# Moving four shared-expert products of one mixture stage behind its tile loop, and their output products into the next stage's routing

## What is computed

```python
# f0: 8 experts of width 176, 2 chosen per token, shared expert of width 352
scores = sigmoid(X @ gate_w.T);  _, idx = top_k(scores + router_bias, 2)
w = take(scores, idx) / sum;     out = sum_e gate[:, e] * (silu(X@W1[e]) * (X@W3[e])) @ W2[e]
out += (silu(X @ sw1.T) * (X @ sw3.T)) @ sw2.T        # the shared expert, for all tokens
x = x + 0.5 * f0(layernorm(x))
# h: gate = sigmoid(f); state scan along the sequence; x = x + (g * rms * norm * silu-like(o)) @ Wo
# f1: as f0 with 16 experts of width 128 and a shared expert of width 128
```

## Time and profile before

| what | us |
|---|---|
| three runs | 949.8, 949.8, 943.32 |
| their median | 949.8 |
| the profiled execution | 945.97 |
| span of its trace | 944.1 |
| mean granted PE clock of that span | 0.924 |

### The profile page before, as it was taken

How to read it: one execution, slowest core, us unless ns; L and a number is a source line. 1 busy time by engine, 2 the same in 40 slices (tenths; PEclk the granted TensorE clock), 3 DMA queues, 4 the chain that set the end, 5 groups by cost and what they waited for, 6 DMA issues and landing times.

```text
span 944.1 us, 14250 instructions
## 1 busy us (share of the span) xinstructions
PE 787.2 (83%) x3838; PEld 546.5 (58%) x3838; DVE 500.4 (53%) x1733; ACT 415.8 (44%) x1021; POOL 300.9 (32%) x312
## 2 busy tenths in 40 slices
PE   5899999978798899899963788895889985789892
PEld 2346677654464347677641367784667664367772
DVE  3656222277765556222287642238777776642238
ACT  3622333325643622334345244452657776145550
POOL 0562433400000651434306624450030033624550
PEclk9999999989998999999975798997899998799997
DMA  8734233199999223232293243436000011244428
GB/s 290 228 117 124 95 100 97 62 325 360 343 342 321 78 84 106 95 113 84 77 384 130 91 148 120 129 111 197 0 1 2 1 46 45 89 145 125 150 95 278
DMA packets 102363, 135.24 MB, mean 143 GB/s; under 512 B 11366, under 2 KB 90726, under 8 KB 101734
## 3 DMA queue, kind: packets, MB, share of 16 engines
q1 hardware_dynamic: 87894, 95.05, 31.4%
q0 software_dynamic: 14400, 39.34, 11.8%
HBM read 56.23 MB, written 78.12 MB: 142 GB/s over the span
## 4 chain that ended last, share of the span: by engine, by line
PE 62%; DVE 11%; issue 8%; ACT 6%; POOL 4%; DMA 4%; another core or an unknown queue 4%; SPq 2%; DVEq 0%; POOLq 0%; ACTq 0%
PE bank L980 18%; PE bank L1001 11%; PE bank L883 5%; PE bank L1050 5%; PE bank L960 4%; PE bank L991 3%; POOL slot_rows L497 3%; PE bank L1099 2%; PE bank L823 2%; PE bank L1140 2%; DVE X L1269 1%; PE bank L1167 1%; PE bank L1125 1%; DVE X L1273 1%
## 5 line engine op out<-in xcount | busy, mean ns | idle before, releaser
L497 POOL DMA_INDIRECT f_result_rows<-arena x172 | 164.8, 958 | 256.3 <-ACT arena L641 157.4
L497 POOL DMA_INDIRECT slot_rows<-XN,slots x128 | 126.1, 985 | 313.7 <-DVE slots L1383 248.7
L980 PE MATMUL bank<-w,arena 128*128 x688 | 208.7, 426 | 0.1
L1582 DVE COPY arena<-bank 88x128 f32<-88x128 f32 (+1 forms) x250 | 65.2, 285 | 249.2 <-PE bank L991 210.0
L980 PEld LDWEIGHTS bank<-w,arena 128*128 128x128 f32 x688 | 132.8, 195 | 32.6 <-issue 1.8
L1001 PE MATMUL bank<-w,arena 88*128 (+1 forms) x500 | 139.7, 388 | 0.0
L883 PE MATMUL bank<-XT,f_s 128*128 128x512 f32 (+1 forms) x256 | 127.8, 651 | 3.4 <-DMA f_s<-in_f_s 1.8
L635 ACT ACTIVATE arena<-bank 128x128 f32<-128x128 f32 (+1 forms) x172 | 50.8, 295 | 122.3 <-PE bank L980 85.9
L641 ACT ACTIVATE arena<-bank 128x256 f32<-128x256 f32 x172 | 66.0, 383 | 82.9 <-PE bank L1001 68.2
L883 PEld LDWEIGHTS bank<-XT,f_s 128*128 128x128 f32 (+1 forms) x256 | 49.9, 203 | 64.9 <-issue 60.5
L1001 PEld LDWEIGHTS bank<-w,arena 88*128 88x128 f32 (+1 forms) x500 | 82.4, 193 | 5.8 <-issue 0.8
(11 more groups left out here) (158 smaller groups left out, 1056.8 us busy)
## 6 DMA issues: line engine op xcount, KB each, us to landing
slot_rows<-zeros SPq DMA_DIRECT2D x16, 2176.0 KB, 17.9
arena<-slot_rows SPq DMA_DIRECT2D x172, 128.0 KB
XN<-f_result_rows SPq DMA_DIRECT2D x32, 256.0 KB, 5.3
Y<-f_result_rows SPq DMA_DIRECT2D x32, 256.0 KB, 6.1
w<-in_f_w SPq DMA_DIRECT2D x1, 4096.0 KB
w<-in_f_w SPq DMA_DIRECT2D x1, 2816.0 KB
f_result_rows<-arena POOLq DMA_INDIRECT x172
X<-in_x SPq DMA_DIRECT2D x4, 512.0 KB, 5.6
```

Source lines behind the costliest of these rows:

```text
L497: pool.indirect_dma_start(out=dst, out_offset=bass.IndirectOffsetOnAxis(ap=idx, axis=0), in_=src, in_offset=None).then_inc(done.sem, 16)
L980: last = pe.matmul(bank[2 + q % 2][:, 0:2 * m.H], xsT[q % 2][:, k, :], L["w13"][:, k, bass.ds(e, 1), :], start=(k == 0), stop=(k == KD - 1))
L1582: last = dve.tensor_copy(hT[q % 2][0:kp, k, :], bank[4 + q % 2][0:kp, k * P:(k + 1) * P])
```

## The change

Four edits, nothing else; no arithmetic is left out or added.

1. The second wide stage (the one whose next stage is narrow: `spread(s)`) makes pairs 8 to 10 after the tile loop too, so that pairs 8 to 11 stand there. Groups 2 and 3 get banks of their own for their output.
2. The output products of groups 2 and 3 of that stage move into the routing of the narrow stage that follows: PE makes them right after it has turned back the logits of groups 0 and 1. DVE adds them just before it combines groups 2 and 3.
3. POOL's waits in that stage: `up(8)` in place of `up(9)`, and `down(2)` in place of `down(4)`.
4. At the end of both wide stages DVE makes `weights()` before it multiplies the held pairs; before the recurrence the adds of groups 2 and 3 both stand after group 0's results have been combined. ACT's table for the square root is asked for by an instruction of its own at the start of the recurrence, and group 0's transposes there go through two banks.

```diff
-        HELD_UP = {len(MOE0.KS): 11, len(MOE1.KS): NG}
+        def spread(s):
+            return s["kind"] == "f0" and s["next"]["kind"] == "f1"
+        def held_up(s):
+            return NG if s["kind"] == "f1" else 8 if spread(s) else 11
         def down_bank(s, g, half):
             held = g - HELD[s["kind"]]
+            if spread(s) and held >= 0:
+                return bank[2 + held + 2 * half]
@@ in_turn (POOL)
-                        pool.wait_ge(*s["up"](9))
+                        pool.wait_ge(*s["up"](8 if spread(s) else 9))
-                        pool.wait_ge(*s["down"](GT))
+                        pool.wait_ge(*s["down"](2 if spread(s) else GT))
@@ recurrence (ACT)
+                act.activation(unused[:, :], epsc[:, :], ACT.Sqrt)
                 loaded(act, "h")
-                    copy_xT(s, 0, t, banks=1)
+                    copy_xT(s, 0, t, banks=2)
@@ mixture (PE)
                     logits_back(s, g)
                     if nk == 1:
+                        if s["prev"]["mixes"] and HELD["f0"] + g < NG:
+                            shared_down(s["prev"], HELD["f0"] + g)
                         positions(s, g)
-                    shared_up(2 * NG)
+                    if not spread(s):
+                        shared_up(2 * NG)
                     tile_lists()
                     pe.wait_ge(*s["experts"](1))
-                    shared_down(0)
-                    shared_up(2 * NG + 1)
-                    shared_up(2 * NG + 2)
-                    shared_down(1)
+                    shared_down(s, 0)
+                    if not spread(s):
+                        shared_up(2 * NG + 1)
+                        shared_up(2 * NG + 2)
+                    shared_down(s, 1)
...
-                for n in range(HELD_UP[nk], NG * nk):
+                for n in range(held_up(s), NG * nk):
                     shared_up(n)
-                for g in range(HELD[s["kind"]], NG):
-                    shared_down(g)
+                if not spread(s):
+                    for g in range(HELD[s["kind"]], NG):
+                        shared_down(s, g)
@@ combine (DVE)
-                if g == late:
-                    shared_add(s, NG - 1)
+                if spread(s):
+                    if g >= HELD["f0"]:
+                        shared_add(s, g)
+                elif g == late:
+                    for held in range(HELD["f0"] if s["kind"] == "f0" else NG - 1, NG):
+                        shared_add(s, held)
@@ mixture (DVE), after the tile loop
-                shared_hidden(HELD_UP[nk], NG * nk)
                 weights()
-                for g in range(HELD[s["kind"]], NG - 1):
-                    shared_add(s, g)
+                shared_hidden(held_up(s), NG * nk)
+                if nk == 1:
+                    for g in range(NG - 1):
+                        shared_add(s, g)
```

More of the change, by code:

```diff
@@ L619, in mixture @@
                 made_already = 2 * NG - 2 if nk > 1 else 0
-                for n in range(made_already, HELD_UP[nk]):
+                for n in range(made_already, held_up(s)):
                     shared_silu(n)
@@ L869, in positions, with shared_down @@
                 last.then_inc(s["pos_psum"].sem, 1)
+            def shared_down(s, g):
+                L = LAYERS[s["kind"]]
+                m = L["m"]
+                nk = len(m.KS)
+                pe.wait_ge(*s["hid"](nk * (g + 1)))
+                for h in range(2):
+                    if g >= HELD[s["kind"]] + 2:
+                        pe.wait_ge(*s["shared_added"](GT * (g - 2) + 2 * (h + 1)))
+                    elif 0 < g < HELD[s["kind"]]:
+                        pe.wait_ge(*s["shared_added"](GT * (g - 1) + 2 * (h + 1)))
+                    for t in (2 * h, 2 * h + 1):
+                        for c, kp in enumerate(m.KS):
+                            last = pe.matmul(down_bank(s, g, h)[:, t % 2 * D:(t % 2 + 1) * D],
+                                             f_HT[0:kp, (g * nk + c) % HTS, t * P:(t + 1) * P],
+                                             L["s2"][0:kp, c, :], start=(c == 0), stop=(c == nk - 1))
+                        last.then_inc(s["down"].sem, 1)
             def mixture(s):
@@ L885, in shared_up @@
                     last.then_inc(s["up"].sem, 1)
[L887 to L899, removed]
                 def tile_lists():
@@ L929, in mixture @@
                         loaded(pe, s["kind"] + "_shared")
-                        if s["prev"] is not None and s["prev"]["mixes"]:
-                            pe.wait_ge(*s["prev"]["shared_added"](NTT))
                     if nk > 1:
@@ L1037, in transpose_group @@
                     for t in range(GT):
-                        transpose_x(s, g, t, banks=1)
+                        transpose_x(s, g, t, banks=2)
                 def project(g):
@@ L1551, in mixture @@
                 if nk > 1:
-                    shared_hidden(2 * NG, 2 * NG + 1)
+                    if not spread(s):
+                        shared_hidden(2 * NG, 2 * NG + 1)
                     copy_lists()
@@ L1556, in mixture @@
                     shared_add(s, 0)
-                    shared_hidden(2 * NG + 1, 2 * NG + 2)
+                    if not spread(s):
+                        shared_hidden(2 * NG + 1, 2 * NG + 2)
                     mark(0, 0, NTT)
-                    shared_hidden(2 * NG + 2, 2 * NG + 3)
+                    if not spread(s):
+                        shared_hidden(2 * NG + 2, 2 * NG + 3)
                     shared_add(s, 1)
```

2 lines of the change are left out of this document (added).

## The result

The changed kernel took 955.11 us in the median of 20 runs (944.79 to 959.42), the kernel before 946.11 (939.73 to 950.67). The ratio is 1.0089, 95% interval 1.0069 to 1.0110: slower by 8.4 us (6.5 to 10.4), within what was predicted. The ratio is taken over fast runs alone, which leaves out two slow ones of the changed kernel (959.1 and 959.42). The join to the narrow stage costs more than the join to the recurrence gives.

What follows compares the result with a forecast made beforehand. Bound by chains of waits at three short places (overall 62% PE, 11% DVE); -2.6 + 1.0 + 9.2 = +7.6 us gave 953.6 from the profiled execution, 957.4 from the median; 955 taken, range 946 to 962.

Steps and rivals of the forecast that it cites:

- The sum: Whole kernel: -2.6 at the recurrence, +1.0 at the routing's end, +9.2 at the narrow stage, together +7.6 us.
- signals seen at once: Rival, chance 0.22: POOL's gate opens at 349.8, PE stays warm, ACT sees its logits in time; +3.2, or 951.
- Held pairs, +5.8: Join to the narrow stage: DVE combines group 0 at 481.4, not 475.65, since all four multiplications stand ahead.
- Output product in the gap, +3.4: Narrow stage: group 2's output takes 7.8 from a cold start, so counting the places comes 3.4 later.
- Adds and the third choice: Narrow stage: group 2's adds shift the second choice by 10.6; of DVE's 3.97 idle, shift becomes 8.0 to 10.4.
- +9.2 at the loop: Join to the narrow stage in all: 9.2 later, bounds 8.0 and 13, with no slack in the rest of the routing.
- Join to the recurrence, -2.6: First wide stage to recurrence: combine 0.4 earlier, table load 1.3 off the chain, projections 2.8 earlier; 2.6 kept, bounds 0.4 and 4.
- End of the routing, +1.0: Second wide stage: POOL sees its gate late, PE idles and may start the loop cold; loss 1.0, bounds -2.2 to +2.5.
- Group 3's output in the way too: Rival, chance 0.17: that product runs cold inside POOL's burst in the narrow stage and slows DVE's choice; +12.9, or 961.
- Faster than before: Rival, chance 0.08: the second wide stage's loop begins without a late-signal wait and the gate opens at once; -1.9, or 944.

Runs made afterwards that it cites:

- the kernel without POOL's wait: Changed kernel without POOL's wait for half of the second output product ahead of the last group's third tile, second wide stage: ratio 1.0073 to the kernel before.
- the second trace: The kernel before and the changed kernel, each run again with no edit, one execution each: 939.5 and 947.1.
- The same routing without the join: Changed kernel with the edits at the join to the recurrence undone: ratio 1.0117 to the kernel before.
- the kernel that takes results first: Changed kernel, DVE taking group 0's results and statistics ahead of the multiplies of pairs 10 and 11 behind the second wide stage: ratio 1.0036 to before.
- the join's kernel: Kernel before with the edits at the join to the recurrence alone: ratio 1.001; with the wait for the clearing split as well: 0.9960.
- the first ten traces: Traces of the kernel before, the changed kernel and variants of both, taken on chips other than that of the last four; no time of their own as a set.
- the last four traces: Four kernels on another chip: results first (ratio 1.0036), no POOL wait (1.0073), and two with the clearing split (0.9960, 0.9964).
- The two parts of the first join, run alone: Kernel before with only DVE's new order at the join to the recurrence, or only the early table load; one execution each, projection at 19.8 and 19.5.

## Why the prediction was right, point by point

- **The sum.** +7.6 forecast, +6.6 in the traces, +8.4 measured (6.5 to 10.4). The number came, but not by the forecast's case in full. At three places the two traces show what the rival *signals seen at once* named: POOL's gate opened 0.28 behind PE's half output, PE stayed warm, and ACT saw the third group's logits 0.4 and 1.5 late, not 4.1. That rival's sum was +3.2; the traces missed it by 2.1 in the first part, where the join's gain did not arrive, and by 1.3 in the second. So the sum owes something to misses that cancel. The 955 does too: it was the middle of 953.6 and 957.4, and the median of before turned out 3.7 lower than the three runs showed.
- **Held pairs, +5.8.** +5.7 at the combine, for the reason given: all multiplications stand ahead of it on DVE. Moving the pairs back gave back 7 us; DVE's results ahead of two of them alone gave 3.4 (0.3 to 6.5), against the kernel without POOL's wait in the same runs.
- **Output product in the gap, +3.4.** Mis-sized: places came 7.9 later than before against their loop, so 2.2. I took the cold row of 526.57 whole, but in 485 to 490 the granted clock was back to 0.75. The Trainium skill, "TensorE: Matmul & The Clock Gate", section "HAM oscillation — how this bites in real kernels", advises against matrix work in pieces between waits. The traces agree in direction: 8.30 and 7.05 us for the first product, 5.36 for the second.
- **Adds and the third choice.** Right in its low case. The sum of these rows is 9.3 at the second choice (10.6 forecast) and 6.7 at the third (8.0 to 10.4, less the same 1.3): ACT saw its logits nearly in time, so the 3.97 of DVE's idle time went, less the 1.4 of group 3's adds. On these chips it is no chance of one trace: the third group's copy came 4.1 to 4.5 behind PE's logits in the six traces with both outputs behind the loop, 0.3 to 1.5 in the four with the outputs in the gaps.
- **+9.2 at the loop.** It measured 9.3, of which only 6.8 stands at the last slot scatter. The other 2.5 arises between it and the loop and is not firmly the change's: two kernels with the narrow stage of before, one execution each, had 8.2 there as well. The term was right by this addition.
- **Join to the recurrence, -2.6.** Mis-sized twice. The combine gained 2.9, not 0.4: I put the results' landing at 195.8, from the issue at 189.74 and the median of 6.1 over 32 transfers. That one transfer took 3.1 in the same trace of before, so it had landed at 192.8, 6.1 behind the loop as in the changed kernel:

```profile
Y<-f_result_rows SPq DMA_DIRECT2D x1, 256.0 KB, 3.1
```

  The projection gained 4, and DVE's eight adds end just ahead of it, as forecast. But then the step failed that the gain goes on to the end. I did not ask what is late next on POOL. The page lists the clearing (16 transfers of 2176 KB, 17.9 us each to landing), and I did not work out when it ends. The first slot scatter came 0.6 earlier in the mean, 1.5 in the best pair of traces; the rest of the first part's 2.7 arises between it and the loop.
- **End of the routing, +1.0.** It came out as -2.1 from the first slot scatter to the loop (51.7 and 49.8, where 53.0 and 52.7 were), so the sign was wrong. POOL's gap was 1.66 (2.52 before), its burst went on at 347.77:

```profile
345.15 0.96 POOL L506 DMA_INDIRECT slot_rows<-XN,slots  x1 [0.30 <-issue]
347.77 0.96 POOL L506 DMA_INDIRECT slot_rows<-XN,slots  x1 [1.66 <-issue]
```

  I had forecast that POOL sees the gate late, and it did not. PE's half output ended only at 347.49 (the granted clock was 0.59 and 0.55 from 340 to 348), and POOL went on 0.28 later; 344.86 and 345.14 in the second trace. PE did not go cold at the loop: its granted clock was 1.00 from 348 on. The -2.1 is not firmly the change's, though. The same routing without the join took 55.3, with one output seen late on DVE. And on the other chip, where PE ran out of work for 4.3 and 5.7 us, the forecast's loss did come. Without POOL's wait:

```profile
343.58 1.12 PE L977 MATMUL bank<-ident,arena 128*128 128x128 f32 x4 [5.74 <-DMA arena<-slot_rows]
344.83 2.71 PE L997 MATMUL bank<-w,arena 128*128 x4
```

  The same four instructions take 1.35 at the full clock; the granted clock was 0.53 from 345 to 350. That loop took 104.1, and 102.9 behind the 4.3 of the kernel that takes results first, where all six other wide loops on that chip took 101.4.
- **The rivals.** *Signals seen at once* is also what the other chip showed: no wait in its four traces is put down to an unknown releaser. The ratio of the nearest kernel, the one without POOL's wait, was 1.0073 there, not the 1.005 of 951, which lies within its interval all the same. The changed kernel itself was not run there. *Group 3's output in the way too* did not come: that product ran warm, 5.36. *Faster than before* did not come either; the loops' waits went both ways, whatever the kernel.

## What to carry to other kernels

Work that is held back "behind the loop" is only free if the queue that takes the loop's results doesn't stand behind it: here four multiplications of 0.7 us, each waiting for 3.5 us of PE, kept group 0's combine 5.7 us back, while its inputs had landed. Before counting a gain at a join, look at the next place where each engine and each queue waits, and at what is due there from long before: a clearing of 35 MB with 1 to 2 us of slack cut a gain of 4 to about 1 at the next stage's first scatter. And a wait on a whole resource, where the stage uses half of it, is worth a question of its own: with the wait split, the join's kernel came out 0.4% faster than before, on the one chip where it ran. Before taking a median for one transfer, ask for that transfer.

## What the runs showed of the hardware

**Signals seen late.** On the chips of the first ten traces, engines that wait for PE in a burst of POOL's scatters often go on only after the burst. In the second wide stage ACT's copy of the logits begins 0.1 behind PE for the first two groups, which end outside a burst, and 1.2 to 5.8 behind it for the other two, which end in one. In the second trace of before, PE's logits of the second wide stage end at 310.5, POOL's burst at 313.0, and ACT copies them at 314.57:

```profile
314.57 0.28 ACT L581 ACTIVATE arena<-bank 128x128 f32<-128x128 f32 x1 [4.08 <-remote]
```

In the first trace of the changed kernel such a signal seems to hold the narrow stage's loop back to 9.0 behind the last slot scatter's start, since DVE makes the tile lists behind the multiplication that waits for this copy. The pair's product ended at 533.86, and POOL's burst at 536.80:

```profile
529.83 4.03 PE L910 MATMUL bank<-XT,f_s 128*128 128x512 f32 x9
```

```profile
538.03 0.60 ACT L608 ACTIVATE arena<-bank 128x512 f32<-128x512 f32 x1 [6.98 <-PE bank L910]
```

On the other chip, of the last four traces, the logits' copy comes 0.1 behind PE for all four groups, burst or not. The way from the second to the third choice of the second wide stage is 9.6 there, 13.0 in the second trace of before. The Trainium skill, "TensorE: Matmul & The Clock Gate", section "The cost: per-tile semaphore tail", gives tens of nanoseconds for the signals of a product; the last four traces agree with it as to its size and the other ten, with 1.2 to 5.8 us, don't. Why the chips differ no run shows, nor does one show why a burst delays a signal.

**Scatters that take longer beside DVE.** A scatter's issue on POOL takes 0.96 as a rule, but up to 4.84 where DVE writes the selection matrices (16-bit, 128x2048 from two inputs) beside it; all 27 slot scatters of 1.3 or more in the 14 traces stand beside this instruction. This is the second trace of the changed kernel, POOL and then DVE:

```profile
533.52 4.84 POOL L506 DMA_INDIRECT slot_rows<-XN,slots  x1 [0.30 <-issue]
```

```profile
534.40 2.27 DVE L1484 TENSOR_TENSOR Y<-iota,arena 128x2048 f16<-128x2048 f32 x1
```

It is the last one ahead of the loop, and the loop begins 8.5 behind its start, instead of the 6.1 and 6.3 of before. The two parts of the first join, run alone, have a last scatter of 4.52 and 8.2 there. The run without POOL's wait has a scatter of 3.02 and the one that takes results first one of 2.67. The Trainium skill, "GPSIMD Engine Reference", section "1. Specifications", says that GpSimd shares its SBUF interfaces with VectorE, with contention where a DVE instruction has two SBUF inputs; these rows agree.
